# A pairwise-product recommendation tower on one core: GpSimd waits for the rows of the duo before, in front of every second duo

## What is computed

```python
e = jnp.stack([tbl_0[ids[:, 0]], tbl_1[ids[:, 1]], ...], axis=1)   # 2048 x 32 x 64
p = inputs[:, ids_x, :]
q = inputs[:, ids_y, :]
pw = jnp.einsum('bpi,pij->bpj', p, w)          # 496 pairs, w is 496 x 64 x 64
out = jnp.einsum('bpj,bpj->bp', pw, q)
h = jnp.concatenate([z, dense_ctx], axis=1)    # 2048 x 512
h = jnp.maximum(h @ W_top1 + b_top1, 0.0)
h = jnp.maximum(h @ W_top2 + b_top2, 0.0)
y = h @ W_top3
```

## Time and profile before

| | |
|---|---|
| runs, median of 3 | 956.79 us (955.41 to 956.92) |
| the profiled execution | 953.77 us, its span 952.0 us |
| mean granted TensorE clock in it | 0.941 of full speed |
| TensorE, matmuls | 794.7 us busy |
| VectorE | 594.2 us busy |
| GpSimd | 590.5 us busy |
| DMA queue of GpSimd | 62.3% of 16 engines |

### The profile page before, as it was taken

One profiled execution on the slowest core, in us unless ns is written; L12 is line 12 of the kernel. 1 busy time (PEld: TensorE's weight loads), 2 busy tenths in 40 slices (PEclk: granted clock), 3 DMA queues, 4 the chain that ended last, 5 costly groups with the idle time before them and its releaser, 6 DMA issues.

```text
span 952.0 us, 10237 instructions
## 1 busy us (share of the span) xinstructions
PE 794.7 (83%) x3792; PEld 285.4 (30%) x3792; DVE 594.2 (62%) x512; ACT 196.0 (21%) x333; POOL 590.5 (62%) x612
## 2 busy tenths in 40 slices
PE   0444958988696999999697999999698799999969
PEld 0111213333232333333232333333233233333313
DVE  0132638976595576777585566688586566689930
ACT  1221212211222122211221222211131222210001
POOL 6756775687687566777577467677577567641110
PEclk9967779999799999999799899999799999999979
DMA  7113449998797577999697478888798578886970
GB/s 280 26 41 67 110 89 218 216 200 198 154 231 172 122 154 167 196 198 200 144 229 175 93 160 184 179 192 199 160 217 186 118 161 183 178 175 135 193 160 0
DMA packets 40760, 153.78 MB, mean 162 GB/s; under 512 B 11332, under 2 KB 11716, under 8 KB 28296
## 3 DMA queue, kind: packets, MB, share of 16 engines
q0 software_dynamic: 30208, 117.48, 62.3%
q1 hardware_dynamic: 10504, 35.67, 10.6%
HBM read 52.43 MB, written 0.01 MB: 55 GB/s over the span
## 4 chain that ended last, share of the span: by engine, by line
PE 61%; issue 10%; another core or an unknown queue 9%; POOL 7%; DMA 6%; DVE 4%; ACT 2%; DVEq 0%; POOLq 0%
PE main_ps L329 34%; PE z_ps L353 13%; PE x_ps L384 7%; DMA prod<-prod 6%; POOL emb L233 5%; DVE prod L417 4%; PE x_ps L309 2%; PE main_ps L384 2%; ACT quad_t L451 2%; POOL prod L245 2%; PE main_ps L330 1%; ACT e_t L440 0%; ACT L440 0%; DVEq L154 0%
## 5 line engine op out<-in xcount | busy, mean ns | idle before, releaser
L417 DVE TENSOR_TENSOR prod<-main_ps,quad_t 128x1024 f32<-128x1024 f32 x448 | 522.6, 1217 | 204.5 <-PE main_ps L330 118.0
L233 POOL DMA_INDIRECT emb<-in_tbl,idx x512 | 496.2, 969 | 198.4 <-issue 150.5
L329 PE MATMUL main_ps<-e_t,w_sb 64*128 64x512 f32 x1024 | 500.4, 625 | 91.4 <-DVE prod L417 44.9
L330 PE MATMUL main_ps<-e_t,w_sb 64*128 64x512 f32 x1024 | 500.3, 625 | 0.0
L329 PEld LDWEIGHTS main_ps<-e_t,w_sb 64*128 64x128 f32 x1024 | 184.7, 193 | 360.3 <-issue 227.4
L353 PE MATMUL z_ps<-prod,const_sb 128*32 128x512 f32 x1280 | 175.1, 639 | 28.7 <-DMA prod<-prod 21.9
L330 PEld LDWEIGHTS main_ps<-e_t,w_sb 64*128 64x128 f32 x1024 | 184.8, 193 | 0.0
L245 POOL DMA_DIRECT2D prod<-prod x96 | 94.2, 985 | 126.2 <-DVE prod L417 119.8
L417 DVE TENSOR_TENSOR prod<-main_ps,e_t 128x1024 f32<-128x1024 f32 x64 | 78.1, 1220 | 115.1 <-PE main_ps L330 81.6
L451 ACT ACTIVATE quad_t<-x_ps 32x512 f32<-32x512 f32 x224 | 131.4, 587 | 2.6
L440 ACT ACTIVATE e_t<-x_ps 128x512 f32<-128x512 f32 x64 | 38.3, 598 | 431.8 <-PE x_ps L309 195.9
(11 more groups left out here) (11 smaller groups left out, 24.6 us busy)
## 6 DMA issues: line engine op xcount, KB each, us to landing
prod<-prod POOLq DMA_DIRECT2D x96, 1024.0 KB
w_sb<-in_w SPq DMA_DIRECT2D x65, 512.0 KB
emb<-in_tbl,idx POOLq DMA_INDIRECT x512
w_sb<-in_w SPq DMA_DIRECT2D x1, 1024.0 KB
z_sb<-in_ctx SPq DMA_DIRECT2D x64, 2.0 KB
idx<-in_ids SPq DMA_DIRECT2D x1, 192.0 KB
const_sb<-in_const SPq DMA_DIRECT2D x1, 125.0 KB, 2.0
idx<-in_ids SPq DMA_DIRECT2D x1, 64.0 KB, 2.0
```

Of the source, the lines that this page charges most:

```text
L233: pool.indirect_dma_start(out=emb[:, n % G_SLOTS, s, odd * EMBED:(odd + 1) * EMBED], out_offset=None, in_=tables[f], in_offset=bass.Indire ...
L329: nc.tensor.matmul(main_ps[:, slot, :], w_sb[LOW, u % W_SLOTS, :], even[LOW, 0, :], start=True, stop=True)
L330: nc.tensor.matmul(main_ps[:, slot + 1, :], w_sb[UP, u % W_SLOTS, :], odd[UP, 0, :], start=True, stop=True)\
L417: nc.vector.tensor_tensor(prod[:, s:s + 2, :], main_ps[:, slot:slot + 2, :], e_q, ALU.mult)\
```

## The change

The first gather of every second duo (n = 2, 4, 6, ... 62) now also waits until all 8 gathers of the duo in front of it have landed. There are 31 such waits. Nothing else is touched: the same instructions, in the same order, on all engines.

```diff
                 if n == DUOS and k == 0:
                     pool.wait_ge(idx_in[1], 16)
+                    pool.nop(nofuse=True)
+                if n > 0 and n % 2 == 0 and k == 0:
+
+                    pool.wait_ge(gathered[(n - 1) % G_SLOTS], GATHERS * ((n - 1) // G_SLOTS + 1))
                     pool.nop(nofuse=True)
                 if n >= ahead(n) and k == 0:
```

## The result

| | before | changed |
|---|---|---|
| median, same chip | 956.86 us (955.41 to 958.19, 4 runs) | 970.41 us (969.28 to 973.31, 4 runs) |
| profiled execution, its span | 953.77 us, 952.0 us | 973.31 us, 971.5 us |
| TensorE matmuls busy | 794.7 us | 809.8 us |
| VectorE, GpSimd busy | 594.2, 590.5 us | 594.8, 590.6 us |
| granted TensorE clock | 0.941 | 0.939 |

The recorded ratio is 1.017, with an interval of 1.0131 to 1.0208 (the two medians alone give 1.014): the change is 13.6 us slower. The forecast was 945.2 us, and its range ended at 963. It was wrong in sign.

The account below looks back on a forecast made before the run. TensorE was taken as the bound, its results arriving late in unbroken gather bursts. Pauses +5.4, gains -11.5, -4.5 and -1 sum to -11.6 us: 956.8 to 945.2 us, range 930 to 963.

Parts of the forecast that it names:

- What bounds the kernel: Whole kernel: TensorE busy 83%, 61% of the chain; a GpSimd wait costs only where it makes TensorE or VectorE late.
- Elsewhere ... I take the pauses there to end inside that slack: Rounds 4 to 19 of later tiles: folds and gathers land well before TensorE needs them, so pauses there cost nothing.
- A pause with no fold ahead: In front of duos 2, 4, 6 and 10: each pause 1.3 us, 5.2 us together.
- Zero on the path: The four 1.3 us pauses of duos 2, 4, 6, 10 only shift GpSimd's existing idle time: 0, bound 5.2 us.
- the first tile: First tile's gather bursts: cutting them wins 1 us, at most 8.5, since the gathers' work nearly fills 60.90 to 143.
- The pause of duo 38: Second tile's end, a fold ahead: 6 us of pause makes the next fold usable 2.4 us late.
- The queue gives back 3.6: At duo 38: an emptier DMA queue lands the fold sooner after issue, returning 3.6 of 6 us of pause.
- What the pauses give back: Pauses cut gather bursts, so TensorE's results arrive less late: gains of 11.5, 4.5 and 1 us.
- the tile ends: Bursts of 12 gathers at three tile ends: half of 22.9 us of VectorE waits won, 11.5 us.
- The unit of 245.16: VectorE unit idle 8.77 us for late TensorE results, a delay once in each of three tiles: 1.5 us gain each.
- the pauses cost and give nothing back: Rival, chance 0.31: late results don't depend on gather spacing, folds come late at tile ends; 962 to 971.6 us.
- If they fall and the time stays, the folds were the next bound at once: Check on the changed profile: VectorE's waits for late results fall from 92.1 us but the time does not improve.

Follow-up runs that it names:

- the fifth chip: Unchanged kernel and the one with all 31 waits, rerun with traces on another chip: 897.46 and 948.96 us, ratio 1.0566.
- the thirteen between the borders: Waits only in front of duos 18, 20, 22, 26, 28, 34, 36, 42, 44, 50, 52, 58, 60, against the kernel before: 920.60 us, 1.0261.
- a fill: GpSimd memsets of a scratch row replacing each of the 22 waits, against the kernel before: four 938.75 us, two 911.95 us, one 899.39 us.
- the tile ends alone: Waits only in front of duos 24, 40 and 56, against the kernel before: 896.37 us, 0.9978; again on another chip 897.22 us, 0.9993.

## Why the prediction was wrong, step by step

- **What bounds the kernel: wrong.** I read 7% of the chain for GpSimd as room. Its own timeline said otherwise. These are folds in the kernel before on the first chip, three of five in a row:

```profile
484.82 1.01 POOL L245 DMA_DIRECT2D prod<-prod  x1
...
490.97 1.01 POOL L245 DMA_DIRECT2D prod<-prod  x1
...
497.12 1.01 POOL L245 DMA_DIRECT2D prod<-prod  x1
```

They stand 6.15 to 6.16 us apart with no wait for VectorE in front of them: four gathers at 1.25 us and a fold, which is all that GpSimd does in a round. VectorE needs 4.62 us for the four units of one (its rows of four in a row, "4.62 DVE ... x4"). So GpSimd had no room there. Nor had the DMA engines: in the four rounds from 478.66 to 503.29 their share is 1.00 to 1.08. TensorE was busy for 4.7 to 6.2 us of each 6.15. The late results hid this in the chain: on the fifth chip, without them, GpSimd holds 22% of it in the same kernel. And GpSimd waited for the products of only 33 of 96 folds; in front of the other 63 no such wait stands.
- **"Elsewhere ... I take the pauses there to end inside that slack": the step that failed.** 22 waits have a fold ahead. I priced five of them (duos 14 and 16, 22, 38, 54) at 5.4 us together, and the other seventeen at nothing. The 22 cost 42.6 us. Of the thirteen between the borders I had twelve at nothing, and the thirteen cost 23.4. The slack is real and is about 0.3 us; I took it to be over 4, from TensorE's and VectorE's small waits for folds. A short wait of the consumer tells that the fold comes in time, not how much earlier it could have been later.
- **A pause with no fold ahead, 1.3 us: it is 2.1.** I took it from TensorE's reaction to the landing; GpSimd goes on later. The page of the Trainium skill that I set against it ("DMA: Bandwidth & Descriptors", about 2.0 us of fixed cost) was nearer than my row. "Zero on the path" held on the first chip, where the first tile is even; with no late results the six waits of that tile cost 7.7 us.
- **The pause of duo 38, 6 us, costing 2.4: right in kind.** GpSimd idled 4.53 us, 4.2 more than usual. "The queue gives back 3.6" is borne out at this place: the fold behind the pause was used 7.6 us after its issue in place of 11.7. The price of 2.4 for such a pause is near the 1.9 us that the 22 cost each in the mean, whether they end on a landing or on a fill. What was wrong is the number of places that pay it.
- **What the pauses give back, 17 us: right in kind and too small.** VectorE's "remote" waits fell to 17.7, not to some 65; by the two kinds of chip 38 us came back. Of the tile ends the second did what was said (6.62 + 1.61 us became 3.27); at the other two the late results went, but VectorE still waited, now for TensorE (7.64 became 6.28, 7.04 became 4.38). The unit of 245.16 starts 7 us earlier, at 238.11, and waits 1.46 us in place of 8.77; I took 1.5 us of gain there:

```profile
238.11 4.62 DVE L421 TENSOR_TENSOR prod<-main_ps,quad_t 128x1024 f32<-128x1024 f32 x4 [1.46 <-PE main_ps L334]
...
309.97 1.23 DVE L421 TENSOR_TENSOR prod<-main_ps,e_t 128x1024 f32<-128x1024 f32 x1 [6.28 <-PE main_ps L334]
...
762.80 4.62 DVE L421 TENSOR_TENSOR prod<-main_ps,quad_t 128x1024 f32<-128x1024 f32 x4 [4.38 <-PE main_ps L334]
```

  I had missed the first tile: I took 1 us there and it was about 10, since the first gather of duo 16 loses 13.0 us on the fifth chip (190.40 to 203.35) and only 2.9 on the first.
- **TensorE's clock: a term that is not in the sum.** A late fold also lowers the granted clock, and on the fifth chip 19.5 of the 49.4 us are TensorE's longer work.
- **Sizes:** +5.4 was 51.5, -17.0 was -38.0 (by the comparison of chips), and the sum -11.6 was +13.5. Since both terms were too small, a ratio near 1 hides two large effects.
- **The rivals.** The time lies in the band of "the pauses cost and give nothing back" (962 to 971.6), but its mechanism is wrong: the "remote" waits fell, and by the comparison of chips 38 us came back. That the time lies in the band is luck. That rival named the folds as what comes late, and in this it was right. "If they fall and the time stays, the folds were the next bound at once" was the closest sentence. The estimate from the Trainium skill's page, 62 us for 31 waits of 2.0 us, stood nearer to the pauses' cost (51.5) than my own sum, though the pauses behind folds are longer than 2.0 us, and cost about half of their length.

## What to carry to other kernels

An engine that issues DMAs one after the other is a bound like any other, and its share of the chain doesn't show it while something else is late: look at how far its instructions stand apart and whether it waits for anything in between. Before a pause is called hidden, measure the slack behind it by pauses of known length (here 0.3 us), and take their length from when the next instruction starts, not from the filler's own time; a small wait of the consumer is no measure of it. Look at the DMA share too: where it is at 1, the transfers have as little room as the engine that issues them, and these runs could not tell the two apart. If a wait for a landing is needed, put it some instructions after the issue: the same 31 waits cost 53 us at once and nothing four gathers later.

## What the runs showed of the hardware that was not expected

- The same kernel takes 957 us on one chip and 897 to 898 us on four others. On the one, TensorE's results reach ScalarE, VectorE and GpSimd up to 14 us after it put the matmuls out, in and after bursts of gathers; in no trace from the four other chips does such a wait stand. On the first chip they came 1.43 us per gather after a burst's start in the kernel before, 1.34 to 1.53 in the changed one, and earlier when bursts were cut. What makes them late was not found: no later set fell on such a chip, so whether the tile-end waits alone, or short fixed pauses, would win there was not tried.
- A gather's landing lets GpSimd go on 2.38 us after its issue has ended, with nothing else in the queue, 2.1 more than the usual 0.30; behind a fold it was 4.53 us. TensorE, released by the same landing, reacts sooner. In the changed kernel the issue of duo 1's last gather ends at 23.59, TensorE starts on the duo at 25.20 and GpSimd goes on at 25.98:

```profile
25.20 1.11 PE L313 MATMUL x_ps<-const_sb,emb 128*128 128x128 f32 x4 [5.56 <-DMA emb<-in_tbl,idx]
```

- A fold that TensorE waits for is used 7.6 us after its issue behind a pause (513.57 to 521.12 in the changed kernel), and 12.9 us after it in a stretch without pauses (465.65 to 478.54 in the kernel before on the fifth chip).
- TensorE's granted clock is 0.50 behind a wait of 3.27 us for a fold, and 8 summing matmuls take 1.94 us there in place of 1.06.
- No version here beats the kernel before: the best, the tile ends alone, is at 0.9978 [0.9951, 1.0005] and 0.9993 [0.9973, 1.0013], which can't be told from it.
